# Counting graph edges in blocks of 625 instead of 640, with the self-loops as ordinary edges and the count table stored in long rows

## The reference, cut to what matters

```python
x = x + L0_gnn(layernorm(x), ...)   # attention over edges, 4 heads, scaled by edge weight
x = x + L0_ffn(...)                 # 2 of 8 experts
x = x + L1_gnn(...)                 # agg = segment_sum(x[src] * edge_weight, dst)
x = x + L1_ffn(...)
x = x + L2_gnn(...)                 # three gat_conv, softmax over the edges of a node
x = x + L2_ffn(...)
x = x + L3_gnn(...)                 # two hypergraph convolutions, the same weighted sum
x = x + L3_ffn(...)
```

## Time and profile before

| | us |
|---|---|
| three runs, median | 5315.39 |
| profiled execution, its own time | 5335.05 |
| span of the profile | 5333.4 |
| busy: PE / DVE / ACT / POOL | 4296.5 / 2421.6 / 1830.3 / 865.0 |
| mean granted TensorE clock | 0.873 |

### The profile page before, as it was taken

One profiled execution on the slowest core, in us unless ns is written; L12 is line 12 of the kernel. 1 busy time (PEld: TensorE's weight loads), 2 busy tenths in 40 slices (PEclk: granted clock), 3 DMA queues, 4 the chain that ended last, 5 costly groups with the idle time before them and its releaser, 6 DMA issues. The chain is left out here.

```text
span 5333.4 us, 81280 instructions
## 1 busy us (share of the span) xinstructions
PE 4296.5 (81%) x23903; PEld 3811.4 (71%) x23904; DVE 2421.6 (45%) x4340; ACT 1830.3 (34%) x3016; POOL 865.0 (16%) x797
## 2 busy tenths in 40 slices
PE   2688878984557989695998999899399959989676
PEld 2577768984347975584887787788299949989554
DVE  5455554784432021214896897797511140020323
ACT  1433311343221014242665665565244310110222
POOL 2677750000440010120000000000122200000101
PEclk8688885896788989797999999999599979999888
DMA  3454422895243310231111111110222133233000
GB/s 94 113 116 116 112 59 58 149 182 96 79 118 125 154 47 24 91 100 55 53 59 40 46 57 40 46 59 35 62 73 84 51 115 154 99 119 152 39 18 26
DMA packets 328368, 441.65 MB, mean 83 GB/s; under 512 B 206704, under 2 KB 270917, under 8 KB 311876
## 3 DMA queue, kind: packets, MB, share of 16 engines
q1 hardware_dynamic: 293028, 342.80, 22.3%
q0 software_dynamic: 35232, 97.61, 6.5%
HBM read 343.94 MB, written 96.35 MB: 83 GB/s over the span
## 5 line engine op out<-in xcount | busy, mean ns | idle before, releaser
L2518 PE MATMUL p_acc<-p_H,p_eT 125*125 125x256 f32 x3750 | 823.5, 378 | 0.0
L2518 PEld LDWEIGHTS p_acc<-p_H,p_eT 125*125 125x125 f32 x3750 | 695.2, 187 | 106.0
L1094 POOL DMA_INDIRECT p_message<-edge_table,p_index x425 | 493.0, 1160 | 151.5 <-issue 120.4
L1316 PE MATMUL p_acc<-p_message,p_spread 125*125 125x260 f32 x1666 | 426.0, 423 | 29.0 <-issue 29.0
L2004 DVE BATCH_NORM_STATS2 features_stats<-F x60 | 29.2, 486 | 891.4 <-ACT F L1995 889.9
L1316 PEld LDWEIGHTS p_acc<-p_message,p_spread 125*125 125x125 f32 x1666 | 348.4, 211 | 98.8 <-issue 31.0
L1751 PEld LDWEIGHTS p_up<-p_xT,p_w1s 128*128 128x128 f32 x3056 | 375.6, 198 | 50.7 <-issue 32.7
L1751 PE MATMUL p_up<-p_xT,p_w1s 128*128 128x125 f32 x3056 | 383.1, 282 | 32.5 <-issue 13.8
L1775 ACT ACTIVATE p_hid<-p_up,p_b1s 128x125 f32<-128x125 f32 x764 | 272.8, 366 | 393.6 <-PE p_up L1751 350.1
L1759 PE MATMUL p_down<-p_w2s,p_hid 128*125 128x256 f32 x1528 | 361.0, 385 | 7.0 <-ACT p_hid L1775 5.8
L1368 POOL IOTA p_order_i<- 125x200 int32 x3 | 1.1, 382 | 2062.8 <-SPq L85 2062.8
(11 more groups left out here) (492 smaller groups left out, 7364.3 us busy)
## 6 DMA issues: line engine op xcount, KB each, us to landing
sums_first<-edge_sums SPq DMA_DIRECT2D x48, 1250.0 KB
p_second<-edge_sums SPq DMA_DIRECT2D x48, 1250.0 KB, 6.7
p_count<-edge_counts SPq DMA_DIRECT2D x75, 762.9 KB
edge_sums<-p_sums SPq DMA_DIRECT2D x32, 1250.0 KB, 10.7
edge_counts<-p_total SPq DMA_DIRECT2D x32, 546.9 KB
p_w1s<-in_L_ffn_W SPq DMA_DIRECT2D x16, 1024.0 KB
p_got<-made SPq DMA_DIRECT2D x25, 560.0 KB
p_dst_all<-dst_row SPq DMA_DIRECT2D x25, 531.2 KB, 4.1
```

The costliest lines, as they stand in the source:

```text
L1094: pool.indirect_dma_start(message[:, m, k, :], None, table, bass.IndirectOffsetOnAxis(ap=index[:, m, k:k + 1], axis=0)).then_inc(landed[m] ...
L1316: last = pe.matmul(at, spread[:, k], message[0:P, m, k], start=(k == 0), stop=(k == R_CH - 1))
L2518: last = pe.matmul(acc[:, s, 0:C], eT[:, r % 4, a % 4], H[:, a, 0:C], start=(a == 0), stop=(a == T - 1))
```

## The change

Blocks are counted in 625 = 25 x 25: `KB` 5, `BG` 25, so a group is 125 nodes, 25 groups, 125 batches. Each block loads 120 edge rows (`OWN`) instead of 128; the lanes 120 to 124 hold its five self-loops (of the first 125 blocks) as edges of weight 0, written once by VectorE in `attend_edges`, and the identity matmuls are gone. `low` and `heavy` are 128 columns wide, `cell` 125; there are five slots instead of four. TensorE makes a batch's five counts, then its five sums, in two PSUM buffers instead of four.

The count table keeps the order in which it is made: row 125 j + key, column 125 u + l, for group j and the block's place u. So a group's store is rows of 6,250 bytes; `attend_nodes` puts it in order when it loads a tile, by five transfers, one for each destination place in a block, of 25 x 25 pieces of 125 numbers. `aggregate` takes 12 pairs of 125-node groups and one single group. The edge loads are 30 for each of the first 21 rounds, and the first three rounds' loads come behind three `dst_all` loads in a row. `begin_rest` and `pick_rest` run behind round 22, the key operations (`block_keys`) behind round 23, both in `attend_edges`. The rest loop reads and writes whole rows of the sums.

```diff
-KB = 4
-BG = 20
+OWN = 120
+KB = 5
+BG = 25
-GROUPS = -(-N // GD)
+GROUPS = N // GD
-LOADS = 26
+LOADS = 30
+LOADED = 21
@@ aggregate: PE (one more call for the single group, also on ACT and SP)
+            one(PAIRS, PAIRS // 2, 0, 1)
@@ count_edges: DVE, one batch
-                dve.wait_ge(batch_used, n + 1)
-                dve.tensor_tensor(low[:, at], lanes, each(lo), ALU.is_equal).then_inc(low_ready, 1)
-                dve.tensor_tensor(cell[:, at], lanes, each(key), ALU.is_equal).then_inc(cell_ready, 1)
+                dve.wait_ge(batch_summed, n + 1)
+                dve.tensor_tensor(low[:, at], lanes(ROWS), each(own.low, n, ROWS), ALU.is_equal).then_inc(low_ready, 1)
+                dve.tensor_tensor(cell[:, at], lanes(P), each(own.key, n, P), ALU.is_equal).then_inc(cell_ready, 1)
+                weighs(dve, n, k)
@@ count_edges: PE, one batch
-                for q in range(KB):
-                    ...
-                    pe.matmul(acc[0:P, at, 0, q * P:(q + 1) * P], cell[:, at, q], low[:, at, q], start=True, stop=not loops, skip_group_check=True)
-                    if loops:
-                        ...
-                        pe.matmul(acc[0:P, at, 0, q * P + first:q * P + first + BLK], g.ident[0:P, 0:P],
-                                  g.ident[0:P, 0:P].rearrange("p (d h) -> p d h", h=T)[:, :, t], start=False, stop=True, skip_group_check=True)
+                for bank, first, many in PIECES_OF:
+                    for q in range(many):
+                        last = pe.matmul(at_bank[0:P, 0, bank, q * P:(q + 1) * P], cell[:, at, first + q], low[:, at, first + q, 0:P], start=True, stop=True)
+                last.then_inc(batch_counted, 1)
+                ...
+                        last = pe.matmul(at_bank[:, 1, bank, q * P:(q + 1) * P], heavy[:, at, first + q], cell[:, at, first + q], start=True, stop=True)
@@ count_edges: SP, one group
-                    split_rows(sp, table[bass.ds(j * BG, BG)].rearrange("b p l -> p b l"), total[:, m], stored[m])
+                split_rows(sp, counts[bass.ds(j * P, P), :], total[:, m].rearrange("p b l -> p (b l)"), stored[m])
@@ count_edges: SP, the rest
-                old = columns[bass.ds(group * ROWS, P), :, bass.ds(place * BLK, BLK)]
+                old = weights[bass.ds(group * ROWS, P), :]
@@ attend_edges: SP
-            over_groups(sp, one)
-            one(ROUNDS - 1, ROUNDS // SETS, 0)
+            for m in range(SETS):
+                one(m, 0, m)
+            sp.wait_ge(loops_made, 4)
+            for r in range(SETS):
+                blocks_of(r)
+            with sp.Fori(1, LOADED // SETS) as i:
+                for m in range(SETS):
+                    one(i * SETS + m, i, m)
+                    blocks_of(i * SETS + m)
+            for r in range(LOADED, ROUNDS):
+                one(r, r // SETS, r % SETS)
@@ attend_edges: DVE
-            begin_rest(dve, rest_then, g, over, over_i, rests)
-            pick_rest(dve, rest_then, g, over)
+            dve.memset(own_blocks.edges[96:128].bitcast(F32), 0.0).then_inc(loops_made, 1)
+            ...
+            def one_and_blocks(r, i, m, coming):
+                one(r, i, m, coming)
+                ...
+                if coming == 2:
+                    ...
+                    begin_rest(dve, then, g, over, own_blocks.spare_i[0:1], own_blocks.spare[0:1, 0:1])
+                    pick_rest(dve, then, g, over)
+                if coming == 1:
+                    dve.wait_ge(own_edges_loaded, 16 * HELD)
+                    block_keys(dve, then, own_blocks, based)
@@ attend_nodes: SP
-                sp.dma_start(count[:, k % 3], counts[nodes(t), :]).then_inc(count_ready[k % 3], 16)
+                own_counts = counts[nodes(t), :].rearrange("(d h) (u l) -> d u h l", d=BLK, u=BG)
+                for d in range(BLK):
+                    sp.dma_start(count[d::BLK, k % 3].rearrange("u (h l) -> u h l", h=T), own_counts[d]).then_inc(count_ready[k % 3], 16)
```

More of the change, by code:

```diff
@@ L716, in _, with one @@
             pe.sem_inc(loaded[0], 32)
[L718 to L719 removed]
+            def one(r, i, m, groups=2):
+                pe.wait_ge(loaded[m], i * 32 + groups * 16)
                 for h in range(KH):
@@ L766, in pick_rest, with __init__ @@
     then(dve.tensor_copy(g.pick_i[:, 0:1], g.pick[:, 0:1]))
-def count_edges(nc, g, edges, own, counts, weights):
-    SLOTS = 4
-    BANKS = 4
-    PER = BG
-    with Phase(nc) as ph:
[L775 to L786, removed]
+class Blocks:
+    def __init__(self, XT):
+        first, second = XT[:, 0], XT[:, 1]
+        self.edges = first[:, 0:4 * HELD].bitcast(I32).rearrange("p (b k) -> p b k", k=4)
+        self.lane = first[:, 4 * HELD:4 * HELD + ROWS]
+        self.lane_i = first[:, 4 * HELD + ROWS:4 * HELD + 2 * ROWS].bitcast(I32)
+        at = [second[:, k * BLOCKS:(k + 1) * BLOCKS] for k in range(5)]
+        self.low, self.key, self.base, self.spare = at[0:4]
+        self.base_i = at[1].bitcast(I32)
+        self.spare_i = at[4].bitcast(I32)
@@ new lines, in block_keys @@
+def block_keys(dve, then, own, based):
+    src, dst = (own.edges[:, 0:BLOCKS, k] for k in (1, 0))
+    then(dve.tensor_copy(own.spare, src))
+    then(dve.tensor_scalar(own.base, own.spare, 4195.0, None, ALU.mult))
+    then(dve.tensor_copy(own.spare_i, own.base))
+    then(dve.tensor_scalar(own.spare_i, own.spare_i, 19, None, ALU.arith_shift_right))
+    then(dve.tensor_copy(own.base, own.spare_i))
+    then(dve.scalar_tensor_tensor(out=own.low, in0=own.base, scalar=-float(P), in1=own.spare, op0=ALU.mult, op1=ALU.add))
+    then(dve.tensor_copy(own.spare, dst))
+    then(dve.scalar_tensor_tensor(out=own.spare, in0=own.spare, scalar=float(T), in1=own.base, op0=ALU.mult, op1=ALU.add))
+    dve.wait_ge(based, 2)
+    then(dve.tensor_copy(own.base, own.base_i))
+    then(dve.tensor_tensor(own.key, own.spare, own.base, ALU.subtract))
+    then(dve.tensor_copy(own.lane, own.lane_i))
@@ L821, in count_edges, with over_batches @@
         block = ph.block()
-        SETUP = 11
         REST = 18
[L824 to L828, removed]
+        old_sums = sums[0:P, 1]
+        def over_batches(eng, one):
+            with eng.Fori(0, BATCHES // PER) as i:
                 for k in range(PER):
                     one(i * PER + k, k, i)
+            for n in range(BATCHES // PER * PER, BATCHES):
+                one(n, n % PER, n // PER)
@@ L832, in rest_total, with each @@
         def rest_total(eng):
             return eng.value_load(g.pick_i[0:1, 1:2], min_val=1, max_val=CH)
[L835 to L840, removed]
+        def each(of, n, wide):
+            return of[:, bass.ds(n * KB, KB)].unsqueeze(2).to_broadcast([EB, KB, wide])
@@ L853, in _ @@
[L853 to L859, removed]
+            dve.sem_inc(batch_summed, SLOTS)
```

184 lines of the change are left out of this document (104 added, 80 removed).

## The result

The new kernel takes 5191.87 us at the median (5187.29 to 5195.46, four runs), the kernel before 5313.08 beside it: ratio 0.9772, 95% interval 0.9755 to 0.9789, 121 us faster. The forecast was 5169 with a range of 5110 to 5250. The profiled executions differ by more: 5335.05 before and 5195.46 after, 139.6 us.

A forecast was written before the change was run, and what follows sets the result against it. Counting was taken as bound first by TensorE at the low clock, then by the count-table store. Stage end -125 and aggregations -21 gave -146 us: 5335.05 to 5189 profiled, 5169 at the median, range 5110 to 5250.

The forecast's parts named there:

- The clock: Counting loop: clock rises a few microseconds after the dense matmuls begin, instead of 0.50 for 157.3 us; about 2 us lost.
- Rival 3: Counting loop: a long start, not small matmuls, held the clock low; +77 us, 5246, or never rising +259, 5428; chance 0.07.
- The store: Counting loop: a group's 2.38 MB in long rows take 6 us at 400 GB/s, hidden in 11.1 us a group.
- Rival 1: Counting loop: stores still bind, 13.1 us a group instead of 11.1; +50 us, 5219; chance 0.08.
- The start of the loop: Counting loop: edge attention ends 25 us later, old set-up saves 11.5, so the first `low` comes at 827 instead of 813.5.
- the keys: End of edge attention: key operations moved behind round 23 put 4.5 us on the path, bounds 0 and 7.5.
- The tail: From the counting loop's last copy to the next stage: 41 us, 4 us more than before.
- the aggregations: Three aggregations: 12 pairs at 21.1 us and one single group at 10.9, 264 instead of 271; together -21 us.
- The node attention: Three node attentions: count loads of 250-byte pieces take 9.6 us a tile, hidden under 13.54; cost 0.
- rival 2: Node attention: count loads bind if a piece costs over 21.7 ns; at 46 ns +1140 us, about 6310; chance 0.08.
- The last step: Whole kernel: carries the 19.7 us between the old profiled execution and median over to the new kernel, 5189 to 5169.
- Rival 4: Start and path pieces: SP's order costs nothing or path pieces are smaller; -25 us, 5144; chance 0.09 beyond the forecast's range.

The follow-up runs named there:

- the first try: New kernel with the 5-column identity matmuls back behind the first 125 blocks' counts, the ten sums passes still together: 5224.08 us.
- the second traces: Kernel before, unchanged, profiled again: 5335.89 us, span 5334.2; paired with a second trace of the new kernel, whose run the text does not specify.
- the later comparisons: New kernel, unchanged, with more runs beside the kernel before: 5198.64 us against 5340.09, ratio 0.9736; before took 5340 to 5343 across the experiments.

## Why the prediction was right, and where it was off

**The clock** (first half of the old loop) was right, and two experiments show it from both sides: -89.7 us by taking the small matmuls out of the old kernel, +100.6 by putting them into the new one in the old order, both with the small matmuls' own time. Rival 3, a long start, falls with that. The reason as it stood, "the small matmuls", was too wide: the first try has all of them and its clock rises. It is their place between all the large ones.

**The store** was right: 328 GB/s where mostly counts go out, against 87, and the wait gone; short stores alone bring back 53.6 us. Rival 1 falls. The two parts and the batch of 2.19 us gave a loop of 281.2 us for the 283 forecast.

**The start of the loop** is the term of the sum that came out most off: +13.5 us was forecast for the first `low`, +21.4 came between the first two traces. Not all of it is a miss. GpSimd's last gather, +15.7 forecast, is +20.7 there (751.11 to 771.76), but +15.8 between the second traces (756.14 to 771.95). The wait at the start was sized right (+16.2); the first pair adds further waits for TensorE (48.3 - 36.9 = 11.4 us instead of 29.0 - 20.7 = 8.3) and slower gathers (495.1 us instead of the earlier trace rows's 493.0). No mis-sizing of this piece is shown.

What both pairs show is the end. From the last gather to the first `low` -2.5 us was forecast (4.5 + 4.5 - 11.5), and +0.8 and +1.2 came. The mis-sized term is the keys: 4.5 us forecast between bounds of 0 and 7.5; from the end of the visit before them to the final operations of the stage (793.89 to 817.76, before 769.19 to 785.26) are 23.9 us instead of 16.1, so 7.8, just above the upper bound. TensorE had matmuls beside them for 5.9 us, and its standstill of 4.80 us is what was forecast. What the forecast put at nothing there is the clock: behind the standstill it was at 0.50, and the last 34 matmuls took 10.44 us (10.45 in the second trace) instead of 7.30, 3.1 us more. The smaller pieces: `begin_rest` and `pick_rest`, 4.5 forecast, took 780.08 - 753.99 - 20.7 = 5.4; the visit behind them gave 1.4 back (13.8 us from 780.08 to 793.89, before 15.2), as TensorE was at the lower clock for some 3 us there instead of 6 (mean clocks of 0.90 over 16.7 us and 0.88 over 25.6); the -11.5 us of the old set-up came as -11.1.

**The tail** (41 forecast, 39.6) and **the aggregations** (21.1 us a hundred passes; 21.11 from start to start, -7.9 and -13.4 us for the layers in the two places) were right. That the next stage begins 120.8 us earlier (124.4 between the second traces) where 125 was forecast is in part luck: the later start was made up by a shorter loop and tail.

**The node attention** at no cost was right, and rival 2 falls with a margin that is now measured: 8.9 us in 13.54. Loading the 250-byte pieces moves 88 GB/s, no more than storing them did (87), but at a DMA share of 0.40 instead of 1.37. So the price of the bulk store, taken on five engines, would have been wrong (28.7 us a tile), and the choice of the nearest load decided this term; on five engines a piece costs 14.2 ns for the 15.4 forecast. The gain is the cover: the pieces' time now lies under TensorE's work. The Trainium skill (DMA: Bandwidth & Descriptors, section "Specifications") gives 512 bytes as the least transfer for line rate and says that the DMA engines read, modify and write below it. The trace agrees on the rate, for loads and stores alike (88 and 87 GB/s, against 328 where mostly rows of 6,250 bytes are stored); no run here shows what the engines do inside. Of the rule for the number of engines that the forecast named, the trace decides nothing: the share through a load is 0.40, five in sixteen would be 0.31 without overlap, and the profile does not name engines.

**The last step** failed: "the difference carried over gives 5169". It took the 19.7 us between the profiled execution of before and its other runs for something that the new kernel has too. Its profiled execution is 3.6 us above its median, and in the later comparisons, where before takes 5340, the new kernel takes 5199. On the profiled execution the sum was 5189 against 5195.46, 6.5 us off; of the 22.9 us by which the median was missed the rest, 16.4, is this step. As a gain, 146 us were forecast; 121 came in the first comparison and 141 in the second. Rival 4, smaller path pieces, was on the wrong side.

## What to carry to other kernels

TensorE can be busy 100% of the time at half its clock: look at the granted clock per stage, and if small matmuls stand between all the large ones, put them elsewhere or group the large ones. A standstill of TensorE can cost more than itself: here 4.8 us of it cost another 3.1 at the lower clock. Where a table must be turned between its maker and its reader, do it where the transfer has cover: loading the short pieces was no faster than storing them here (88 and 87 GB/s), but it fits under the reader's matmuls, and the store had no such room. And when many small loads are put on a queue, put them behind the one load that the next engine waits for: here 25 to 30 us lay in the order of one queue.

## What the runs showed that was not expected

- Sums in a row of ten passes let the clock rise although ten small passes stand in the same batch (1.00 from 880 to 900 us); the same passes one by one between the small ones keep it at 0.50 for all 25 batches.
- Halving the pieces of a load made it 1.4 times as long (12.6 against 8.9 us), not twice and not the same.
- Behind a standstill of 4.80 us TensorE ran at the lower clock for some 6 us, which cost 3.1 us more.
- Two traces of one kernel can differ by 5 us in when the edge attention's last gather goes out (751.11 and 756.14), so that a miss of that size between two single traces is no miss yet.
- The kernel before differs by 27 us between the first comparison and a later one, the new kernel by 7. The cause was not traced.
